# Row maximum and scale in one accumulating VectorE operation, and another deal of the second layer's side pieces

## The reference

```
x = x + tanh(g_xattn[0]) * causal_attention(layernorm(x), ctx, ctx)          # softmax over keys, 16 heads
x = x + tanh(g_ffn[0])   * moe(layernorm(x), 32 experts, top 8)
x = x + tanh(g_xattn[1]) * image_attention(layernorm(x), ctx, w_q, w_k_img, w_v_img, w_o, ...)   # not causal, 256 keys
x = x + tanh(g_ffn[1])   * (layernorm(x) @ ternary(weight).T + bias)
softmax(s)_k = exp(scale*s_k - scale*max_k s_k) / sum_k exp(...)
```

## Time and profile before

| | |
|---|---|
| median of 3 runs | 1507.68 us (1507.03 to 1513.49) |
| the profiled execution | 1504.07 us, its span 1502.3 us |
| PE busy | 1330.9 us, 89% |
| DVE, ACT, POOL busy | 964.9, 927.6, 519.0 us |
| mean granted TensorE clock | 0.978 |
| L344 TENSOR_REDUCE | 256 times, 158.4 us |
| L346 TENSOR_SCALAR | 256 times, 48.2 us |

### The profile page before, as it was taken

How to read it: one execution, slowest core, us unless ns; L and a number is a source line. 1 busy time by engine, 2 the same in 40 slices (tenths; PEclk the granted TensorE clock), 3 DMA queues, 4 the chain that set the end, 5 groups by cost and what they waited for, 6 DMA issues and landing times.

```text
span 1502.3 us, 37766 instructions
## 1 busy us (share of the span) xinstructions
PE 1330.9 (89%) x11005; PEld 837.6 (56%) x11006; DVE 964.9 (64%) x2381; ACT 927.6 (62%) x2269; POOL 519.0 (35%) x532
## 2 busy tenths in 40 slices
PE   4888888958989999999999999677989899898987
PEld 3665566624656666666666666344555555565553
DVE  5888888664545566555655633244787786877764
ACT  4877777724656666666666666334766667566653
...
GB/s 73 29 176 183 156 148 148 178 231 315 270 288 288 262 224 237 264 215 231 229 236 219 184 146 152 131 105 89 103 83 80 107 67 89 96 69 70 2 15 29
DMA packets 96149, 233.42 MB, mean 155 GB/s; under 512 B 11824, under 2 KB 11824, under 8 KB 91440
## 3 DMA queue, kind: packets, MB, share of 16 engines
...
## 4 chain that ended last, share of the span: by engine, by line
PE 44%; DMA 10%; DVE 8%; issue 7%; ACT 3%; POOL 3%; SPq 2%; DVEq 0%; POOLq 0%; ACTq 0%
PE bank L1329 18%; PE bank L1353 10%; PE bank L1586 6%; DMA xs<-y_tiles,slot_ix 6%; PE bank L1317 4%; POOL xs L449 2%; PE bank L277 2%; DMA xg<-x_slots 2%; PE bank L1340 1%; PE bank L297 1%; PE bank L1592 1%; DVE l_nmax L344 1%; DMA x_slots<-blank 1%; ACT l_probs L312 1%; PE bank L259 1%
## 5 line engine op out<-in xcount | busy, mean ns | idle before, releaser
L1329 PE MATMUL bank<-wh,xT 128*128 x1280 | 340.3, 328 | 6.2 <-DVE hp L1445 4.1
L449 POOL DMA_INDIRECT xs<-y_tiles,slot_ix x120 | 192.3, 1603 | 238.2 <-DMA y_tiles<-ysb 98.9
L312 ACT ACTIVATE l_probs<-bank,l_bias 128x256 f32<-128x256 f32 (+1 forms) x512 | 225.1, 451 | 59.5 <-DVE l_bias L346 58.8
L1329 PE MATMUL bank<-wl,xT 128*128 x640 | 209.7, 328 | 0.0
L344 DVE TENSOR_REDUCE l_nmax<-bank 128x2 f32<-128x512 f32 (+1 forms) x256 | 158.4, 619 | 66.6 <-PE bank L259 38.8
L1435 DVE SCALAR_TENSOR_TENSOR hv<-bank,sg 128x192 f32<-128x192 f32 x160 | 57.0, 356 | 222.9 <-ACT sg L1389 200.6
L1404 ACT ACTIVATE ysb<-bank,xg 128x512 f32<-128x512 f32 x160 | 109.9, 687 | 118.3 <-PE bank L1353 118.3
L324 ACT ACTIVATE l_probsT<-bank 128x512 f32<-128x512 f32 (+1 forms) x256 | 140.8, 550 | 67.1 <-PE bank L297 66.7
L1383 ACT ACTIVATE xT<-bank 128x1024 f16<-128x1024 f16 x160 | 162.6, 1017 | 14.2 <-PE bank L1317 13.8
L1329 PEld LDWEIGHTS bank<-wh,xT 128*128 128x128 f16 x1280 | 125.6, 98 | 81.3 <-issue 11.1
L1353 PE MATMUL bank<-wh,hT 128*128 x480 | 156.3, 380 | 0.9 <-issue 0.6
...
...
...
## 6 DMA issues: line engine op xcount, KB each, us to landing
...
```

The costliest lines, as they stand in the source:

```text
L312: last = self.nc.scalar.activation(self.probs[:, s % 2, u, 0:nk], self.pS[s % 2][:, u * S : u * S + nk], ACT.Exp, bias=self.bias[:, s % 4, ...
L449: return nc.gpsimd.indirect_dma_start(to, None, self.y_tiles[0 : (MT + 1 - k) * P, :], ix, compute_op=ALU.add)
L1329: last = nc.tensor.matmul(bGU[t.place % 2][:, 0:GU], xT[:, t.place % 2, xo + c * P : xo + (c + 1) * P], wp[:, bass.ds(w, 1), c * GU : (c + ...
```

## The change

Two things. In `dve_max` the reduction and the small multiplication become, for each of the two heads, one TENSOR_SCALAR that multiplies by -scale, takes the minimum with a huge number, writes the products to a scratch tile `scaled`, and with its accumulator output leaves the minimum of the row (which is -scale times the maximum) in `bias`. The wait between the two old instructions and its semaphore go; a wait for the step before the last stays.

In layer 1 pieces change rows: PE's T2 from 6 to 7, PE's h1 before the pv instead of behind it, DVE's S4 and S5 from 12 to 13, ACT's f1 from 13 to 11, POOL's d1 from 10 to 12. And PE waits, before the scores of a batch's step 0, only for the copy of S5; the wait for S7 comes before the scores of step 8. ACT's `sx` takes over a wait that `sc` had. The loop over pieces in the vector block gains a class of early pieces, of which the tables have none.

```diff
@@ PREP1
-    pe={1: ["T0"], 2: ["<T1", "P0"], 4: ["P1"], 5: ["P2"], 6: ["T2"], 7: ["T3", "P3"], 8: ["<S0", "<S1"],
+    pe={1: ["T0"], 2: ["<T1", "P0"], 4: ["P1"], 5: ["P2"], 7: ["T2", "T3", "P3"], 8: ["<S0", "<S1"],
...
-         9: ["P4", "S2"], 10: ["S3", "r", "k2"], 11: ["P5"], 12: ["k3", "S4", "S5"], 13: ["S6", "S7"]})
+        9: ["P4", "S2"], 10: ["S3", "r", "k2"], 11: ["P5"], 12: ["k3"], 13: ["S4", "S5", "S6", "S7"]},
@@ POST1
-    pe={0: ["a0"], 1: ["a1"], 5: ["<c0", "c1"], 6: ["d0"], 8: ["d1"], 13: ["<g0", "g1"], 14: ["<h0"], 15: ["h1"]},
-    act={1: ["b0"], 4: ["b1", "c0"], 5: ["c1"], 11: ["f0"], 13: ["f1", "g0", "g1"]},
-    pool={10: ["d1"]},
+    pe={0: ["a0"], 1: ["a1"], 5: ["<c0", "c1"], 6: ["d0"], 8: ["d1"], 13: ["<g0", "g1"], 14: ["<h0"], 15: ["<h1"]},
+    act={1: ["b0"], 4: ["b1", "c0"], 5: ["c1"], 11: ["f0", "f1"], 13: ["g0", "g1"]},
+    pool={12: ["d1"]},
@@ pe_step
         if s + 2 < STEPS:
+            if s + 2 == STEPS // 2:
+                pe.wait_ge(*self.copied(b.n, 7))
             self.pe_scores(b, s + 2)
         elif more:
             if s + 2 == STEPS:
-                self.wait_stack(pe, b.next().n)
+                pe.wait_ge(*self.copied(b.next().n, 5))
             self.pe_scores(b.next(), s + 2 - STEPS)
@@ dve_max
-        v = self.pS[s % 2][:, :].rearrange("p (u k) -> p u k", u=2)[:, :, 0:nk]
-        self.nc.vector.tensor_reduce(self.nmax[:, s % 4, :], v, AX, ALU.max).then_inc(self.max_made, 1)
-        dve.wait_ge(self.max_made, STEPS * b.n + s + 1)
-        self.nc.vector.tensor_scalar(self.bias[:, s % 4, :], self.nmax[:, s % 4, :], -self.scale, None, ALU.mult).then_inc(self.bias_made, 1)
+        if s >= 2 or not (isinstance(b.n, int) and b.n == 0):
+            dve.wait_ge(self.bias_made, STEPS * b.n + s - 1)
+        for u in range(2):
+            last = self.nc.vector.tensor_scalar(self.scaled[:, s % 2, u, 0:nk], self.pS[s % 2][:, u * S : u * S + nk], -self.scale, HUGE,
+                                                ALU.mult, ALU.min, accum_out=self.bias[:, s % 4, u : u + 1])
+        last.then_inc(self.bias_made, 1)
@@ act_prep
             if piece == "sx":
                 act.wait_ge(xn_ready, b.n + 1)
+                act.wait_ge(at.stack_ps, 8 * b.n + 8)
...
             elif piece == "sc":
-                act.wait_ge(at.stack_ps, 8 * b.n + 8)
+                act.wait_ge(at.stack_ps, 8 * b.n + 6)
```

More of the change, by code:

```diff
@@ L46 @@
 SC_N = 2.0**10
+HUGE = 3.0e38
 SC_C = 2.0**8
@@ L1941, in body @@
                     at.dve_step(dve, b, s, more, before=do_post)
+                    ahead = [piece for piece in PREP["dve"].get(s, []) if piece.startswith("<")] if do_prep else []
+                    for piece in ahead:
+                        dve_prep_(dve, b.next(), piece.lstrip("<"), prep)
                     for piece in pieces(post_of(b)["dve"], s) if do_post else []:
@@ L1945, in body @@
                         dve_post_(dve, b, piece, post)
-                    for piece in pieces(PREP["dve"], s) if do_prep else []:
+                    for piece in PREP["dve"].get(s, [])[len(ahead) :] if do_prep else []:
                         dve_prep_(dve, b.next(), piece, prep)
```

10 lines of the change are left out of this document (6 added, 4 removed).

## The result

The changed kernel takes 1484.59 us (median of 4 runs, 1484.15 to 1488.71), beside 1507.36 for the kernel before (4 runs). The ratio is 0.9863, with an interval of 0.9833 to 0.9893: 1.4% faster, where 0.68% and 1497.5 us had been forecast, with a range of 1480 to 1513. The profiled execution took 1484.15 us, its span 1482.4; against the 1502.3 of before that is 19.9 us less, and the forecast's sum had 10.2 less.

The account below looks back on a forecast made before the run. PE was taken to bound layer 1, with holes from a train on DVE, and DVE to be near the bound in layer 0. 1504.07 - 13.3 + 3.1 = 1493.9 us, as a median 1497.5; range 1480 to 1513.

Parts of the forecast that it names:

- the middle one: DVE's new maximum: a pipelined accumulator read adds 0.08 us per main part, so 0.03 us more per step.
- the 3.1 us more of the sum: Cost of the new maximum on DVE: 2.0 us in layer 0 plus 1.1 us in layer 1.
- the deal: Layer 1's pieces moved to other rows and the shorter stack wait: 13.3 us less over the bodies together.
- the accumulator costs nothing: Rival, DVE's maximum in both layers: 0.13 us less per step, median 1481.5 us; chance 0.16.
- d1, f1, S4/S5 and the shorter wait: End of a layer 1 body: r starts sooner and step 14 no longer waits for S7's copy; 2.0 us less per body.
- h1: PE's h1 before the pv in layer 1: the output copy comes sooner, 0.54 us less per body.
- T2: PE's T2 in row 7, layer 1: its wait moves to P3, 0.25 us lost per body.
- Body 0's 0.5 (0.6 worked out): Layer 1's body 0 has no f1; with S7's copy off the path it gains some 0.6 us of 1.39.
- The wait that changes hands: Rival, layer 1: gather 11 waits for an earlier gather, making d1's rstd late; median 1503.8 us, no difference; chance 0.15.
- What would show it: List of signs expected in the changed kernel's trace: waits, step pitches, body lengths, and layer 0 longer by 2 to 3 us.
- Layer 0's share: Part of layer 0's 128 steps where the maximum's price counts: at least 38 of 102; 2.0 us taken from 1.4 to 3.8.

Follow-up runs that it names:

- dep_wait: The changed kernel with one wait more: the second TENSOR_SCALAR of a step waits until the first has signalled; 1494.01 us, ratio 0.9912 to the kernel before.
- deal_only: The changed kernel with the old maximum (reduction, wait, small multiplication); 1491.76 us, ratio 0.9888 to the kernel before.
- xc_early: The changed kernel with POOL's xc in row 4 instead of 5, ahead of the gather of step 5; ratio 0.9844 to the kernel before, on a slower chip.

## Why the prediction was wrong, and where it was right

**The step that failed** is the one on the accumulator: "I take the middle one, 0.03 us, since ACT's read is the nearest row". The pitches of the main parts were right (0.33 and 0.20 worked out, 0.34 and 0.21 measured). The read was given a slot of 0.08 us behind each of them, since on ACT the next instruction starts 0.09 behind the read the earlier trace rows. On DVE it starts with the read. So a step became 0.10 us shorter instead of 0.03 longer, and the 3.1 us more of the sum are 8.4 less alone and, on top of the deal, 7.2 less by the medians (1491.76 to 1484.59) or 3.8 by the ratios (0.9888 to 0.9863). That is 10 of the 13 us by which the median came out below the forecast, or 7 of 10 by the ratios. The rival "the accumulator costs nothing" had 1481.5 us for -0.13 per step, near the 1484.6 measured; it was given 0.16 against an analogy between two engines, though DVE's own rows showed that a follower starts before an operation ends. The Trainium skill ("VectorE: DVE Perf Modes", section Two Vector instructions with no wait between them) says that such an operation is two instructions and that one which nothing holds starts before the earlier has finished; the trace agrees in both, with a read of 0.08 us. It gives no price for the pair, and the reading that I gave it, the middle case, was mine.

**The cause behind the sign.** What the change removes, the wait for the reduction to end, was in the sum, but inside the pitch of 0.79 and without a name; I had looked only at what is added, and so took two operations more for a cost. dep_wait measured the wait: 0.12 us. The Trainium skill (same page, section Rules for kernel authors) advises against fusing; here the fused form was faster with 512 instructions more, because it dropped a dependent wait, so the rule did not hold.

**The deal** was right in its parts. Per body, worked out and then measured by undoing each: d1, f1, S4/S5 and the shorter wait 2.0 against 2.46 (0.92, 0.52, 0.15, 0.87); h1 0.54 against 0.70 with the cheap maximum; T2 -0.25 against -0.34. These prices do not add up: their sum is 2.8, while the whole deal takes 2.2 us off body 2 with the cheap maximum (60.13 to 57.91) and 2.6 with the old one (60.90 to 58.32), so they overlap. The deal alone took 2.58 to 2.85 us off bodies 2, 4 and 5 (2.29 worked out) and 1.5 off body 6 (1.2). In body 1 it cost 1.8 us where 2.3 of gain were in the sum. Body 0's 0.5 (0.6 worked out) is luck: step 13, where the shorter stack wait acts, gave 0.75, step 5 another 0.8, and steps 6 and 7 together lost 1.0. Added up, the bodies of deal_only's trace give some 11 us (body 3 without the fall of the clock that it had before) where the sum had 13.3, and the runs 15 to 17; in which stretch the rest of the gain lies is not shown. That the deal's total came out near its forecast is thus in part luck.

**The wait that changes hands** did come, but at another gather: not ahead of d1, which was in time, but ahead of xc in body 1. xc_early shows this place and price (4.9 us: 3.3 in step 5 and 1.7 in step 6, at the lower clock, with 0.1 less elsewhere). The wait was in the kernel before too (0.7 us in step 5 of body 1, 9 in that of body 0), and its rows were there to be read. Why it grew in body 1 and shrank in body 0 stays open: with h1, T2 or the stack wait undone body 1 takes 58.8 to 59.3 us and its step 5 5.2 to 5.9, with d1, f1 or S4/S5 undone 62.4 to 64.4 and 6.8 to 8.1.

**What would show it**, item by item: r directly behind S3, yes; no wait at g1 nor before step 14, yes; 0.7 us before step 13, 0.94 (1.02 with the old maximum, for which it had been worked out); 0.85 at S6, 0.62 (0.83 with the old maximum); the output copy 0.1, none seen; P3 0.8, 0.67; bodies 2, 4 and 5 2.3 shorter, 3.0 to 3.25; pitches 0.82 and 0.56, 0.69 and 0.43; layer 0 longer by 2 to 3 us, shorter by 1 to 4; a fall of the clock before step 13, none there, but one in step 6 of body 1 and two in body 7 and the tail.

**Layer 0's share.** Even with the right price my share would have been too high for a gain: I took half of the 128 steps for a saving, and my 2.0 us for a cost of 0.03 are about half of them too (67); 1 to 4 us of 13.4 are 7 to 30%.
